# A graph layer on one core: three of seven groups of the key softmax go from the opening stage into the message loop, and residual sums stay on chip

## The reference, cut to what matters

```
xn  = layernorm(x)
msg = xn[dst] * (silu(edge_attr @ Wf1 + bf1) @ Wf2 + bf2)     # 100000 rows
agg = segment_sum(msg, src)                                   # 6250 rows
gnn = xn + batchnorm(silu(agg @ Wu1 + bu1) @ Wu2 + bu2)
q, k, v = xn @ Wqkv;  k = softmax(k, over all 6250 nodes)
ctx = k^T v  (8 heads);  gate = sigmoid(gelu(LN(xn) @ Wg1 + bg1) @ Wg2 + bg2)
x2  = x + gnn + (q @ ctx) * gate @ Wproj + bproj
out = x2 + slice_attention(layernorm(x2)) @ W_out + b_out
```

## Time and profile before

| | |
|---|---|
| median of 3 runs | 2218.55 us (2213.65 to 2227.55) |
| the profiled execution | 2221.49 us, its span 2219.7 us |
| mean granted TensorE clock | 0.944 |
| PE busy | 1924.0 us (87%) |
| PE weight loads | 1587.5 us (72%) |
| DVE busy | 1528.4 us (69%) |
| POOL busy | 1441.2 us (65%) |
| ACT busy | 1307.3 us (59%) |

### The profile page before, as it was taken

One profiled execution on the slowest core, in us unless ns is written; L12 is line 12 of the kernel. 1 busy time (PEld: TensorE's weight loads), 2 busy tenths in 40 slices (PEclk: granted clock), 3 DMA queues, 4 the chain that ended last, 5 costly groups with the idle time before them and its releaser, 6 DMA issues. The chain is left out here.

```text
span 2219.7 us, 38972 instructions
## 1 busy us (share of the span) xinstructions
PE 1924.0 (87%) x10218; PEld 1587.5 (72%) x10218; DVE 1528.4 (69%) x3525; ACT 1307.3 (59%) x2330; POOL 1441.2 (65%) x989
## 2 busy tenths in 40 slices
PE   3687999989999989998899989998990785999878
PEld 2466788778877777777777777777780574788678
DVE  6654777777767767776776677767771557999645
ACT  2333776767666667666776676667760463666423
POOL 2111888888888888888888888888885550455300
PEclk9898999999999999999999999999995895999979
DMA  8656888988898888888988888798886880000002
GB/s 276 275 225 204 160 157 153 187 147 149 146 180 155 149 157 169 145 153 158 171 155 151 173 160 155 141 184 156 143 132 121 263 277 0 1 0 0 20 20 97
DMA packets 288441, 325.45 MB, mean 147 GB/s; under 512 B 29575, under 2 KB 251178, under 8 KB 288146
## 3 DMA queue, kind: packets, MB, share of 16 engines
q0 software_dynamic: 112896, 102.81, 37.7%
q1 hardware_dynamic: 169568, 216.13, 30.9%
q10 hardware_dynamic: 5746, 3.90, 0.7%
HBM read 167.64 MB, written 154.97 MB: 145 GB/s over the span
## 5 line engine op out<-in xcount | busy, mean ns | idle before, releaser
L903 POOL DMA_INDIRECT sums<-summed,out_idx x784 | 1238.8, 1580 | 295.7 <-issue 208.3
L957 PE MATMUL bank<-wf,hidT 128*128 128x256 f32 x3136 | 802.0, 384 | 0.0
L957 PEld LDWEIGHTS bank<-wf,hidT 128*128 128x128 f32 x3136 | 547.2, 192 | 54.7
L1048 ACT ACTIVATE hidT<-bank,bf 128x512 f32<-128x512 f32 x392 | 269.8, 688 | 265.4 <-PE bank L935 222.3
L1143 DVE TENSOR_TENSOR msg_low<-msg,msg_high 128x512 fp32r<-128x512 f32 x392 | 271.9, 694 | 175.0 <-ACT msg_high L1068 129.0
L1174 DVE TENSOR_TENSOR msg<-bank,gathered 128x512 f32<-128x512 f32 x392 | 269.2, 687 | 117.6 <-PE bank L957 91.6
L1068 ACT ACTIVATE msg_high<-msg 128x512 fp32r<-128x512 f32 x392 | 247.3, 631 | 92.2 <-DVE msg L1174 79.1
L955 PE MATMUL bank<-gnn_bf_halves,ones 128*128 128x256 f32 x784 | 298.2, 380 | 0.0
L1056 ACT ACTIVATE summed<-pair 128x516 f32<-128x516 f32 x392 | 230.3, 588 | 61.6 <-DMA sums<-summed,out_idx 59.1
L1075 ACT ACTIVATE gathered<-bank 128x512 f32<-128x512 f32 x392 | 231.9, 592 | 49.8 <-issue 22.3
L945 PE MATMUL bank<-window,spread 128*128 128x256 f32 x784 | 194.6, 330 | 62.6 <-DVE spread L1138 38.3
(11 more groups left out here) (324 smaller groups left out, 2823.4 us busy)
## 6 DMA issues: line engine op xcount, KB each, us to landing
window<-xn_halves SPq DMA_DIRECT2D x392, 128.0 KB
sums<-gate SPq DMA_DIRECT2D x32, 800.0 KB, 10.1
id_row<-id_rows SPq DMA_DIRECT2D x98, 256.0 KB
attr<-attr_rows SPq DMA_DIRECT2D x98, 256.0 KB
part<-sums SPq DMA_DIRECT2D x48, 512.0 KB, 6.6
xn_halves<-xn_halves SPq DMA_DIRECT2D x7, 1792.0 KB, 6.6
id_row<-id_rows SPq DMA_DIRECT2D x98, 128.0 KB
sums<-summed,out_idx POOLq DMA_INDIRECT x784
```

The costliest lines, as they stand in the source:

```text
L903: nc.gpsimd.indirect_dma_start(g.sums_dram[k], bass.IndirectOffsetOnAxis(ap=out_idx[:, ET * c + t:ET * c + t + 1], axis=0), summed[c % 2][ ...
L957: mm = T.matmul(out, hidT[:, j // 2, f, ds((2 * (j % 2) + t) * P, P)], g.wf2[:, f, :], start=False, stop=f == CB - 1)
L1048: A.activation(hidT[:, h, f, :], hps[:], ACT.Silu, bias=g.bf1[:, f:f + 1]).then_inc(hid_ready, 1)
```

## The change

1. The opening makes keys, exponentials and gram of groups 0 to 3 only (`EARLY = 4`). It still normalises, transposes, halves and stores all seven. The fold into `wqm` leaves it.
2. The message loop gets a lead of 14 chunks, written out, in which `prepare(q, place)` does groups 4, 5 and 6, each in 18 places: keys, which ACT copies to SBUF so that two banks of PSUM suffice, maxima, two places with exponentials, transposes, gram, the addition at place 17. x is loaded again at place 0 and normalised in `res_stage`. The fold is done at place 54 and at places 1 and 3 of output group 0.
3. The output work of a group now has 48 places (12 chunks) in place of 56; gelu, gate, query and projection stand closer together.
4. `xT` is laid out by group and shares its memory with the residual sums `g.res`: the sum of group s is written where the transposed rows of group s stood, which are read for the last time before. The stores to DRAM and the reload in `update_nodes` are gone.
5. Where two tiles share a bank, one bias matmul of 512 columns stands for two of 256 (filters, projection, last stage).

```diff
@@ opening
             for k in range(NG):
                 turn_x(k)
...
-                if k:
+                if 1 <= k <= EARLY:
                     turn_e(k - 1)
-                k_product(k)
+                if k < EARLY:
+                    k_product(k)
...
-                else:
+                elif k <= EARLY:
                     gram_group(k - 1)
-            turn_e(NG - 1)
-            gram_group(NG - 1)
...
-            pe.wait_ge(gram_added, NG)
-            for f in range(CB):
-                for b in range(CB):
-                    mm = T.transpose(g.ps[0][:, ds(b * C + f * P, P)], gram_acc[:, f, ds(b * P, P)], g.ident[:])
...
@@ places
-PLACES = 4 * 14
-AT_STORE, AT_LOAD = 0, 4
-AT_HIDDEN = (6, 8)
-AT_SUM = (12, 13, 14, 15)
-AT_GATE = (24, 28, 32, 36)
-AT_QUERY = (26, 30, 34, 38)
-AT_PROJ = (42, 45, 48, 51)
+EARLY = 4
+LEAD = 14
+LATE_PLACES = 18
+AT_KEYS = (0, 1, 2, 3)
+AT_EXP = (6, 7)
+AT_ROWS = (5, 6, 7, 8)
+AT_TURN = (8, 10, 12, 14)
+AT_GRAM = (10, 12, 14, 16)
+AT_ADD = 17
+AT_FOLD = 54
+AT_CTX, AT_WQM = 1, 3
+PLACES = 4 * 12
+AT_LOAD = 3
+AT_HIDDEN = (5, 7)
+AT_SUM = (10, 11, 12, 13)
+AT_GATE = (20, 23, 26, 29)
+AT_QUERY = (21, 24, 27, 30)
+AT_PROJ = (34, 37, 40, 43)
...
+        for n in range(LEAD):
+            chunk(n // 2, n % 2, False, lambda q: prepare(*divmod(4 * n + q, LATE_PLACES)))
@@ SP
-            def store_res(s):
-                sp.wait_ge(res_ready, 4 * s + 4)
-                sp.dma_start(split_rows(g.res_dram, s * GT, GT), res[:]).then_inc(res_out, 16)
...
+            def prepare(q, place):
+                if place == 0 and q < NG - EARLY:
+                    k = EARLY + q
+                    n = GT - 1 if k == NG - 1 else GT
+                    if q:
+                        sp.wait_ge(gram_made, k)
+                    sp.dma_start(res[:, 0:n, :], split_rows(g.x_dram, k * GT, n)).then_inc(x_in, 16)
...
@@ PE, filters
+                T.matmul(fps[j % 2][:], g.ones2[:], for_tiles(g.bf2, 2), start=True, stop=False)
                 for t in range(2):
                     out = fps[j % 2][:, ds(t * C, C)]
-                    T.matmul(out, g.ones2[:], g.bf2[:], start=True, stop=False)
...
@@ PE, lead
+            def keys(q, j):
+
+                k, h, f = EARLY + q, j // CB, j % CB
+                if j >= 2:
+                    pe.wait_ge(keys_copied, 4 * q + j - 1)
+                elif q and j == 0:
+                    pe.wait_ge(e_ready, 4 * k)
+                elif q:
+                    pe.wait_ge(gram_added, k)
+                for b in range(CB):
+                    mm = T.matmul(bankKeys[j % 2][:, 0:HC], g.wqkv[:, b, ds(C + f * P, P)],
+                                  g.xT[:, ds((CB * k + b) * GC + h * HC, HC)], start=b == 0, stop=b == CB - 1)
+                mm.then_inc(k_made, 1)
...
+            def gram_rows(q, n):
+
+                k = EARLY + q
+                pe.wait_ge(e_ready, 4 * k + n + 1)
+                pe.wait_ge(presum_ready, 4 * q + n + 1)
...
@@ ACT, lead
+            def copy_keys(q, j):
+                h, f = j // CB, j % CB
+                n = tokens_in(EARLY + q, h)
...
+                act.wait_ge(k_made, 4 * (EARLY + q) + j + 1)
+                A.activation(e_col[:, f, ds(h * HC, n)], bankKeys[j % 2][:, 0:n], ACT.Copy).then_inc(keys_copied, 1)
...
+            def expo(q, h):
+
+                k = EARLY + q
+                if h == 0:
+                    act.wait_ge(maxed, k + 1)
+                    act.wait_ge(keys_copied, 4 * q + 4)
+                    act.wait_ge(sum_step, SUM_STEPS * (k - 1))
+                    A.activation(fade[k % 2][:], fade_log[:], ACT.Exp).then_inc(faded, 1)
+                for f in range(CB):
+                    cols = e_col[:, f, ds(h * HC, tokens_in(k, h))]
+                    A.activation(cols, cols, ACT.Exp, bias=g.neg_max[k % 2][:, f:f + 1],
+                                 accum_out=k_part[k % 2][:, f, h:h + 1]).then_inc(k_exp, 1)
...
@@ DVE, lead
+            def prepare(q, place):
+                if q * LATE_PLACES + place == AT_FOLD + 1:
+                    dve.wait_ge(sum_step, SUM_STEPS * NG)
+                    V.reciprocal(k_inv[:], g.k_tot[:]).then_inc(fold_ready, 1)
+                    dve.wait_ge(mat, MAT_DONE + 1)
+                    V.tensor_copy(gram[:].rearrange("p b n -> p (b n)"), bankT[:]).then_inc(fold_ready, 1)
+                elif q < NG - EARLY:
+                    if place - 2 in AT_KEYS:
+                        maximum(q, AT_KEYS.index(place - 2))
+                    if place - 2 == AT_KEYS[-1]:
+                        maxima(q)
+                    if place in AT_ROWS:
+                        normalise_rows(q, AT_ROWS.index(place))
+                    if place - 1 in AT_TURN:
+                        copy_e(q, AT_TURN.index(place - 1))
+                    if place == AT_ADD:
+                        add_group(q)
...
@@ residual sum
-                    V.tensor_tensor(res[:, here, :], bankK[:, 0:len(tiles) * C].rearrange("p (t c) -> p t c", c=C),
+                    V.tensor_tensor(g.res[:, ds(s * GT + tiles[0], len(tiles)), :], bankK[:, 0:len(tiles) * C].rearrange("p (t c) -> p t c", c=C),
                                     res[:, here, :], ALU.add).then_inc(res_ready, 1)
@@ update_nodes
-            sp.dma_start(g.res[:, 0:half, :], split_rows(g.res_dram, 0, half)).then_inc(res_in, 16)
-            sp.dma_start(g.res[:, half:NT, :], split_rows(g.res_dram, half, NT - half)).then_inc(res_in, 16)
```

More of the change, by code:

```diff
@@ L168, in opening @@
     neg_group = sb("neg_group", [P, CB], F32)
-    neg_max = [sb(f"neg_k_max{k}", [P, CB], F32) for k in range(2)]
     fade_log = sb("fade_log", [P, CB], F32)
@@ L688, in bias_row, with for_tiles @@
     return halves
+def for_tiles(row, n):
+    return row[:].unsqueeze(1).to_broadcast([BIAS_ROWS, n, C])
 def is_first(v):
@@ L856, in output @@
             def output(s, place):
-                if place == AT_STORE and not is_first(s):
-                    store_res(s - 1)
                 if place == AT_LOAD:
@@ new lines, in gram_rows @@
+            def gram_rows(q, n):
+                k = EARLY + q
+                pe.wait_ge(e_ready, 4 * k + n + 1)
+                pe.wait_ge(presum_ready, 4 * q + n + 1)
+                for t in pair_tiles(n):
+                    rows = rows_of(k * GT + t)
+                    for f in range(CB):
+                        mm = T.matmul(bankK[:, ds(f * C, C)], e_node[0:rows, t, ds(f * P, P)], res[0:rows, t, :],
+                                      start=t == 0 and f == 0, stop=t == GT - 1 and f == CB - 1, skip_group_check=True)
+                if n == 3:
+                    mm.then_inc(gram_made, 1)
@@ L999, in output @@
             def output(s, place):
+                if is_first(s) and place in (AT_CTX, AT_WQM):
+                    fold(1 if place == AT_CTX else 2)
                 if place in AT_HIDDEN:
```

257 lines of the change are left out of this document (175 added, 82 removed).

## The result

The kernel after takes 2250.2 us (median of 4 runs, 2248.4 to 2250.9) against 2219.9 us (4 runs) for the kernel before: a ratio of 1.0134, 95% interval 1.0101 to 1.0167. It is slower by 1.3%. The forecast was 2225 us (2214 to 2238), the range 2198 to 2254; slower by over 1% had a chance of 0.24. The profiled span grew from 2219.7 to 2248.2 us, by 28.5.

What follows compares the result with a forecast made beforehand. The prediction took POOL's scatters to bound the message loop. From the 2218.55 us median, -9 (opening) +19 (lead) +2 (fold) -6 (DMA) = +6 gave 2225 us, range 2198 to 2254.

Steps and rivals of the forecast that it cites:

- Opening, -9: Opening: with three groups' key work gone, the next block starts 9 us earlier (4 to 14), with stores and clears ending last.
- some 20 us: Opening: the gain possible were there no DMA, which the table clears were said to cover.
- Lead, +19: First 54 loop steps: three late groups take 228 us where POOL took 208.8, so 19 us lost (1 to 54).
- 76 us a group: Lead: time of PE, ACT and DVE together for 18 steps, 54 base plus 15.6 PE work plus 6.5 exponentials and waits.
- 6.5 us a group for exponentials and tables: Lead: cost of both exponential places, table loads and small waits to PE, ACT and DVE together, 1 to 18 us.
- The first rival: Lead nearly free, as exp brings no table loads or they hide, and PE's work fits under POOL: 2207 us, chance 0.27.
- The second rival: Lead starves POOL deeply, delays passing between three engines; at 4.7 us a step it costs 45 us: 2253 us, chance 0.23.
- Fold, +2: Loop after the lead: fold into `wqm` and first two gelus take 47.5 us against POOL's 45.5, 2 us lost.
- The dropped stores, -6: Output groups: seven residual stores leave and three loads come, giving back some 6 us (2 to 12) at POOL.
- Output groups of 48 places, 0: Output groups: same work in fewer steps, 3.5 to 3.6 us against POOL's 3.79, costs 0 us, up to 8.
- the forecast's own mechanism: Whole kernel: the change does what the forecast says, 2225 us within 2214 to 2238, chance 0.42.

Runs made afterwards that it cites:

- Run 5: Kernel after, with the 32 table clears put behind the stores of groups 0 to 3 and none behind the last three: 2230.2 us, ratio 1.0037.
- empty lead: Kernel after, with keys, exponentials, turns, gram rows and row loads of the three late groups left out: 2215.5 us, ratio 0.9982.
- run 1: Kernel after, with Tanh in place of Exp in the three late groups' exponentials: 2231.5 us, ratio 1.0043.
- Run 4: Kernel before, without its seven stores of the residual rows; the update stage reloads x rows instead: 2218.5 us, ratio 0.9992.
- run 3: Kernel before, with output groups of 48 places in place of 56, begun 14 chunks later: 2225.4 us, ratio 1.0021.
- run 7: Kernel before, with only the filter's two bias products of 256 columns merged into one of 512: ratio 1.0003.
- run 9: Kernel after, with VectorE's low attribute row subtraction moved behind the two small index instructions of its step: 2257.2 us, ratio 1.0162.
- 11: Kernel after, with VectorE's low attribute row subtraction moved ahead of the low half of the messages: 2250.1 us, ratio 1.0128.
- 12: The kernel of run 10, with the low attribute row subtraction moved ahead as in run 11: 2218.0 us, ratio 0.9983 to the kernel before.
- 8: Kernel after, with five groups in the opening, two late ones over 27 steps each, exponentials together, clears early: 2219.6 us, ratio 0.9994 to before.
- 10: The kernel of run 8, with the six stores of filter weight parts issued behind group 4's store: 2215.2 us, ratio 0.9973 to the kernel before.

## Why the prediction was right in its first three steps and short in its size

**Opening, -9.** Measured -9.7; gate scale at 178.3 for a forecast of 178.4. The step was right, as was the reason: the clears end last. Run 5 shows it by moving them away: the block then starts 21.9 us earlier still. The "some 20 us" that the text put under their cover were meant for the opening as a whole; both changes together gave 31.4, and by the estimate at run 5 some 11 of these were to be had without the shorter opening.

**Lead, +19.** Measured +21.6 from POOL's 208.8 and +26.2 from the 204.2 us of an empty lead. The front's 76 us a group were 78, 74 and 76. Of the parts, 6.5 us a group for exponentials and tables, the loads with what comes with them measured 17.5 / 3 = 5.8 (run 1). The sum had PE at full clock; the lead had 13.6 us at the lower level. That the sum held all the same is in part luck. The first rival, a lead nearly free, had as its condition that exp brings no loads; run 1 meets the condition with a lead of 212.9 us where the rival had 210, so its sum was sound and its condition false. The second rival, 4.7 us a step, did not come: PE's late work cost 8.7 us in three groups on top of POOL's pace, so hand-overs over three engines don't multiply it here.

**Fold, +2.** Measured +2.4.

**The dropped stores, -6.** This step failed. I had laid a wait of 1.61 us at scatter 109 and a quarter of each group's excess over bare scatters to the store and load that run there. Run 4 takes the stores away and the rest stays within 0.6 us. What the profile named for that wait were earlier scatters' DMAs. The store had been issued at 399.75 us, 21 us ahead of scatter 109, the load of x at 412.57, 8 us ahead; I gave the credit to the one that leaves. The dear stretch falls on the load, which stays in all kernels; whether the load makes it is open. The sum was loose too: (1.90 - 1.84) x 112 is 6.7 us and not 6, and a quarter of that in seven groups is 12 us, or 7 if the three new loads are taken off.

**Output groups of 48 places, 0.** This step failed too. The front was to take 3.5 to 3.6 us a step and took 3.84 to 3.86 in groups 1 to 4 without being held, which is above the 3.79 that I had for POOL. The forecast came from output group 0 of the kernel before, whose copies never stood 8 us apart at a turn. That cost little, because the front had got ahead of POOL in its first output group, at 3.67 us a step: the mean lag fell from 14.6 to 11.6 us over groups 1 to 5. And the scatters did not stay as they were. Of the 10.5 us, packing alone in the kernel before gives 6.0 (run 3), though 3.5 of these as idle time. Of the other 4.5 the empty lead has 2.4, and 2.1 appear with the late work, less than kernels with the same loop differ by (1244.1 to 1247.5). Neither the merged filter bias (run 7) nor the stores (run 4) are in it. What else differs there is the residual written to its place for good, the rows' layout, and where loads fall; none was tried alone. The cause of these 4.5 us stays open.

What makes a scatter long is shown in part. Counted over the timelines of POOL and DVE in the rest, a scatter of the kernel after took 1.75 us or more in 35 of the 50 cases in which VectorE's `redirect` was at work 0.4 to 0.6 us behind the scatter's start, against 70 of 652 overall (before: 18 of 53, against 32 of 652). `redirect` need not be the one that does it: in three of four steps it follows right behind VectorE's 0.69 us subtraction `msg_low`, and of the scatters that started within 0.4 us behind the start of `msg_low` 51 of 70 were long (before: 20 of 29). That these meetings are 70 in the one kernel and 29 in the other goes along with the difference in long scatters. Moving one VectorE instruction by one or two places changed the rest by 5 to 9 us in three of three trials (runs 9, 11, 12), in the first two mostly through the durations, in the third through idle time. That VectorE's order reaches into the rest is shown, and into the scatters' durations clearly by run 9 alone; through what it does so is not shown, and which order is good I could not tell ahead: both moves made it worse.

**The tail.** 3.7 us more than before after the last scatter; in the fourteen kernels it varies from 517.0 to 523.3 us with the same code in the stages there, apart from the bias and the reload. I can't assign it.

With -9.7 + 21.6 + 2.4 in place of -9 + 19 + 2, and 0 in place of -6, the sum would have been +14; the rest's 10.5 and the tail's 3.7 make the measured 28.5. The measured 2250 us lies in the range of 2198 to 2254, but above the 2214 to 2238 that the forecast's own mechanism had. The range reached so far only for the second rival, at 2253, whose 4.7 us a step did not come: that the time fell inside is luck.

## What to carry to other kernels

A loop that one engine's fixed-cost instructions bound has the room that its front shows per step, no more: ask for the added work's pace in each step, count its function-table switches first (here two thirds of the lead's cost, with the lower clock that came with them), and spread it thin, as runs 8 and 10 do. Before work is moved out of a stage, look at what else ends there: here DMA stood idle early in the stage and was full at its end, and the order of the clears was worth 21.9 us once the work had left, the work itself 9.5. A transfer is not a wait's cause because it runs beside it; leave it out and look, and where two run there, leave out each.

## What the runs showed that I had not expected

- Which functions stand side by side matters: silu and tanh ran without a load between them (run 1), exp between silus took two loads of 1.28 us. A load with what came with it was worth 1.46 us on this path, and the lower clock is part of that.
- The same scatter instruction lasts 1.54 us mostly, and 1.75 to 2.05 us in 5 to 12 of 100 cases in the rest; the sum of its durations differed by 10 us between two kernels whose POOL idle times agree to 0.1 us.
- With the queues' clears out of the way the opening was 21.9 us shorter, more than twice what removing three groups of PE's work from it had given by itself. Part of that, 11 us by estimate, would have come in the kernel before too.
